# Score tiles in three places in the last steps, and a copy in place of a transfer for the last pair

## The chip, the cores and the metric

The kernel runs on one core of one Trainium2 chip. The metric is the device time of the whole program in microseconds (us). A core has TensorE (PE), VectorE (DVE), ScalarE (ACT), GpSimd (POOL) and SyncE (SP), each with a queue of its own that works strictly in program order. They meet only at semaphores. PE writes to PSUM, eight banks of 128 partitions by 512 float32.

## The reference

One transformer layer on a graph of 4096 nodes, with 128 channels, 8 heads of 16 and a hidden layer of 512. In each head every node attends to the nodes that the adjacency matrix marks.

```python
qkv = layer_norm(x, g1, be1) @ w_qkv                 # x: 4096 x 128
q, k, v = qkv.reshape(n, 3, HEADS, HEAD_DIM)[:, 0..2]
scores = einsum('nhd,mhd->hnm', q, k) * SCALE        # 8 x 4096 x 4096
attn = softmax(where(adj != 0, scores, -inf), axis=-1)
out = einsum('hnm,mhd->nhd', attn, v).reshape(n, DIM)
x = x + out @ w_proj + b_proj
h2 = layer_norm(x, g2, be2)
return x + gelu(h2 @ w1 + b1) @ w2 + b2
```

## The kernel before

**Tiling.** The queries are worked in 8 tiles of 512 (`TILES`), the heads in 4 pairs, the keys in 32 blocks of 128. A tile has 64 steps (`STEPS`): 16 steps for each pair, two key blocks in each step (`BLOCKS`, `block_of`). `run_iterations` runs `body(i, ...)` for i = 0 to 8; body 8 holds only what is left of tile 7. Its flags say what a body still does: b (there is a next tile), c (there is a tile), d (there was one before). Tile 7 has b false; body 8 has b and c false.

**A block.** PE writes the mask into two PSUM banks with four matmuls against an identity (`masks`, L1210), adds the scores of both heads with four matmuls (`scores`, L1225), ACT takes the exponential of both banks in one instruction (128x1024) into one of eight slots of `probs` (L794), and three steps later (`LAG`) PE multiplies by the values and adds up in `pv_ps` (`weigh_values`, L1118). In every odd step the first block is not masked by PE: POOL multiplies its exponentials with 0 or 1 (`mask_probs`, L565), and `weigh_values` waits for that.

**The scores' ring.** `score_ps` has four banks, two halves of two banks. All uses of it, blocks and small fills, are numbered as places (`SCORE_PLACE`, `ACT_PLACE`). The half is the place's number modulo 2, and PE waits in `score_turn` until ACT has taken the place two before (L1106). The fills are small products that ACT reads: the new queries, the shifts (the parts of the row maxima, L669), the second norm's transpose and the four up-projections. Which fills a body has depends on its flags: tile 7 has the shift fill of step 45, but not those of steps 53 and 61, and their places stay empty.

**The rows' ring.** `ring_ps` has three banks. PE writes row scores there (`row_scores`, L1054), DVE adds the adjacency row and takes the maximum (`row_maximum`, L832): four units in each step, 21 steps ahead of their use (`AHEAD`). So tile 7 has none in its steps 43 to 63. Some fills that DVE reads use this ring too. In tile 7 the last of them comes in step 38, and the next in step 5 of body 8.

**Order on PE in a step.** Two row units, then masks of both blocks and scores of both blocks (in an odd step: scores, masks, scores), two row units, an odd step's score fill, the weighing of three steps earlier, an even step's score fill, a row fill.

**Values of a pair.** When a pair's 16 steps are weighed, ACT copies `pv_ps` (`take_values`, L758): for an even pair to `halves[:, 0]`, for an odd one to `attn`. `move_values` then starts transfers from ACT's queue: for the even pair the upper 64 partitions go to `halves[0:64, 1]` (L764), for the odd pair both parts of `attn` go to `halves[64:128]` (L767, L768). POOL adds the two halves into `attn` (`sum_values`, L628) after `values_moved` has counted three transfers. For tile 7's last pair this happens in body 8, steps 3 and 5, and the rest of the layer follows in series: sums (L1152), reciprocals (L932), their broadcast (L1159), projection (L1167), second norm on DVE, transpose (L1137), up (L1142), Gelu (L749), down (L1176), output.

```python
for bank, to, (source, keys) in (...):
    last = nc.tensor.matmul(bank[to, :], ident_bf[keys, keys], mask_t[keys, source, :], start=True, stop=False)
last.then_inc(masks_set, 1)
```

Of the kernel before, what the change touches and what calls it, by code (L numbers as in the profile page):

```python
# [21 lines left out]
TILES = N // TILE  # L22
# [9 lines left out]
PAIRS = HEADS // 2  # L32
# [134 lines left out]

SCORES = Ring(0, ("score", SCORE_PLACE), ACT_PLACE, SCORE_PLACES)
ROWS = Ring(FIRST_UNITS, ("row", ROW_PLACE), DVE_PLACE, ROW_PLACES)


KEPT = [m for m in range(MB) if m % 4 == 3]
# [2 lines left out]
def pool_masked(p, m):  # L175

    return m in KEPT
# [62 lines left out]
def program(nc, x, adj, w_qkv, w_proj, b_proj, w1, b1, w2, b2, g1, be1, g2, be2, const, out):  # L240
    with ExitStack() as ctx:
# [132 lines left out]
        def made(ring, i, bcd, place):  # L374

            return ring.before(i) + ring.upto(bcd, place)

        def free(ring, i, bcd, place, turn):

            held = [p for p in ring.held(*bcd) if p <= place - turn and (place - p) % turn == 0]  # L380
            if bcd[1]:
                return made(ring, i, bcd, place - turn)
            return made(ring, i, bcd, held[-1]) if held else ring.before(i)

        block = ctx.enter_context(nc.Block())

# [101 lines left out]
        def _(pool):  # L488
# [134 lines left out]

            def sum_values(n, f):

                pool.wait_ge(values_moved, (n // 2) * (16 * 3))
                settled(pool)
                nc.gpsimd.tensor_tensor(attn[:, f, :], halves[:, 0, :], halves[:, 1, :], ALU.add).then_inc(attn_ready, 1)  # L628

# [35 lines left out]
        def _(act):  # L665
# [55 lines left out]

            def take_fill(i, par, bcd, g, what):

                half = 2 * (ACT_PLACE[g] % 2)
                bank = score_ps[:, half, :]
                act.wait_ge(score_full, made(SCORES, i, bcd, ACT_PLACE[g]))
                if what[0] == "q":
                    if bcd[2]:
                        act.wait_ge(gelu_done, i * FC)
                        act.wait_ge(q_stored, i * 32)  # L730
                    nc.scalar.copy(q_high[:, :], bank)
                    nc.scalar.copy(q_x[:, :], bank).then_inc(score_taken, 1)
                elif what[0] == "shift":
                    store_shift(q_stack[par if what[1] else 1 - par], bank, what[1], what[2]).then_inc(score_taken, 1)
                elif what[0] == "h2t":
                    nc.scalar.activation(h2T[:, :], bank, ACT.Identity, scale=gb[:, 2:3],  # L736
                                         bias=gb[:, 3:4]).then_inc(score_taken, 1)
                elif what[0] == "up" and bcd[1]:
                    f = what[1]
                    n = (i - 1) * FC + f  # L740
                    if f == 0:
                        act.wait_ge(q_done, min(i, TILES - 1))
                    if f >= 2:
                        act.wait_ge(gelu_done, n - 1)
                    nc.scalar.activation(hidden[:, f, :], bank, ACT.Identity, bias=b1_col[:, f:f + 1])
                    nc.scalar.activation(bent[f % 2], bank, ACT.Square, bias=b1_col[:, f:f + 1])\  # L746
                      .then_inc(score_taken, 1)
                elif what[0] == "up":
                    nc.scalar.activation(hidden[:, what[1], :], bank, ACT.Gelu_apprx_tanh,  # L749
                                         bias=b1_col[:, what[1]:what[1] + 1]).then_inc(score_taken, 1)  # L750
# [9 lines left out]
            def move_values(n, p):  # L760
# [4 lines left out]
                else:  # L765
                    act.wait_ge(values_moved, (n // 2) * (16 * 3) + 16)
                    act.dma_start(halves[64:128, 0, :], attn[64:128, p // 2, :]).then_inc(values_moved, 16)  # L767
                    act.dma_start(halves[64:128, 1, :], attn[0:64, p // 2, :]).then_inc(values_moved, 16)  # L768

            def body(i, par, b, c, d):  # L770
                bcd = b, c, d
                fills = fills_of(ACT_FILLS, b, c, d)
                for g in range(STEPS):
                    if g == X_STEP and d:
                        act.wait_ge(row_taken, ROWS.before(i))
                        act.dma_start(x_res[:, :, :], tile_of(x_view, i - 1)).then_inc(x_res_in, 16)
                    if b and g == XQ_STEP:
                        src = xnT_dram[i + 2] if isinstance(i, int) else \
                            xnT_dram[bass.ds(i + 2, 1)].rearrange("a p n -> p (a n)")
                        act.dma_start(xq[:, :], src).then_inc(xq_loaded, 16)  # L780
                    if d and g == LAG:
                        take_values(i * PAIRS - 1, PAIRS - 1, i * STEPS)
                        if not c:
                            move_values(i * PAIRS - 1, PAIRS - 1)
                    if c and g % QUARTER == LAG and g > QUARTER:
                        take_values(i * PAIRS + (g // QUARTER - 1), g // QUARTER - 1, i * STEPS + (g - LAG))
                    for n in range(BLOCKS):
                        if c:
                            if g >= SLOT_STEPS or not (isinstance(i, int) and i == 0):
                                act.wait_ge(pv_done, i * STEPS + (g - SLOT_STEPS + 1))  # L790
                            place = SCORE_PLACE[g, n]
                            act.wait_ge(score_full, made(SCORES, i, bcd, place))
                            half = 2 * (place % 2)
                            nc.scalar.activation(probs[:, (2 * g + n) % SLOTS, :],  # L794
                                                 score_ps[:, half:half + 2, :].rearrange("p a n -> p (a n)"),
                                                 ACT.Exp, scale=score_scale[:, 0:1]).then_inc(score_taken, 1)
                            if n == 0 and g % QUARTER == LAG and (g > QUARTER or d):

                                move_values(i * PAIRS + (g // QUARTER - 1), (g // QUARTER - 1) % PAIRS)
                    if g in fills:  # L800
                        take_fill(i, par, bcd, g, fills[g])
                    if d and c and g - 2 in UP_STEPS:
                        f = UP_STEPS.index(g - 2)
                        act.wait_ge(bent_done, 2 * ((i - 1) * FC + f) + 2)
                        nc.scalar.activation(bent[f % 2], bent[f % 2], ACT.Tanh).then_inc(tanh_done, 1)
                    if d and g == STORE_STEP:
                        act.wait_ge(row_taken, made(ROWS, i, bcd, DVE_PLACE[34]))
                        act.dma_start(tile_of(out_view, i - 1), rows2[:, :, :]).then_inc(out_stored, 16)
                    if d and g == SEEN_STEP:
                        act.wait_ge(out_stored, i * 16)  # L810
# [205 lines left out]
        def _(pe):  # L1016
# [85 lines left out]

            def score_turn(i, bcd, place):

                if place >= 2 or not (isinstance(i, int) and i == 0):
                    pe.wait_ge(score_taken, free(SCORES, i, bcd, place, 2))  # L1106

            def weigh_values(i, bcd, g):
# [14 lines left out]

            def act_fill(i, bcd, g, what):
                place = ACT_PLACE[g]
                bank = score_ps[:, 2 * (place % 2), :]
                score_turn(i, bcd, place)
                if what[0] == "q":
                    pe.wait_ge(xq_loaded, (i + 1) * 16)
                    last = nc.tensor.matmul(bank, wq_all[:, :], xq[:, :], start=True, stop=True)  # L1130
                elif what[0] == "shift":
                    pe.wait_ge(split_step, SPLIT_OPS * (neg_max_order(i + (what[1] == 0), what[1], what[2]) + 1))
                    last = transpose_shift(bank, what[2])
                elif what[0] == "h2t":
                    pe.wait_ge(ln2_applied, (i - 1) * (SUB + 1) + SUB)
                    for s in range(SUB):
                        last = nc.tensor.transpose(bank[:, 128 * s:128 * (s + 1)], rows2[:, s, :], ident[:, :])  # L1137
                elif what[0] == "up":
                    f = what[1]
                    if f == 0:  # L1140
                        pe.wait_ge(score_taken, made(SCORES, i, bcd, ACT_PLACE[H2T_STEP]))
                    last = nc.tensor.matmul(bank, w1_sb[:, 128 * f:128 * (f + 1)], h2T[:, :], start=True, stop=True)  # L1142
                last.then_inc(score_full, 1)
# [36 lines left out]
            def body(i, par, b, c, d):  # L1180
# [13 lines left out]
                def block(g, n):  # L1194

                    p, m = g // QUARTER, block_of(g, n)
                    half = 2 * (SCORE_PLACE[g, n] % 2)
                    return p, m, score_ps[:, half, :], score_ps[:, half + 1, :], pool_masked(p, m)

                def masks(g, n):  # L1200

# [86 lines left out]
```

## Time and profile before

| | us |
|---|---|
| median of 3 runs | 1713.71 (1713.29 to 1714.76) |
| the profiled execution | 1713.18 |
| its span | 1711.4 |
| PE busy | 1592.9 (93%) |
| DVE busy | 1418.5 (83%) |
| ACT busy | 1275.2 (75%) |
| POOL busy | 1167.7 (68%) |

The span is the time from the first to the last recorded instruction of one profiled execution. The profile has the mean exponential at 1112 ns, and its sections on 40 slices show PE at 9 tenths or more from the second slice to the last but two. A releaser in an arrow (`<-`) is what ended an engine's idle time.

### The profile page before, as it was taken

What the parts mean: (1) busy time and instruction counts of PE and PEld (TensorE: products, weight loads), DVE (VectorE), ACT (ScalarE), POOL (GpSimd) and SP (SyncE); (2) the same over time, 40 slices, a digit from 0 to 9 for tenths busy, and PEclk for the clock granted to TensorE, in tenths of its full rate; (3) what the DMA queues carried; (4) which work ended last, traced back from release to release, by engine and by line L of the source; (5) the groups of instructions that cost most, each with busy time, mean ns of one, the idle gap of its engine ahead of it and who ended that gap; (6) DMA issues with size and microseconds to landing.
All of it is one profiled execution on the core that took longest, in us unless ns stands there. A gap on an engine that the chain in (4) does not pass through costs nothing.

```text
span 1711.4 us, 46526 instructions
## 1 busy us (share of the span) xinstructions
PE 1592.9 (93%) x17016; PEld 496.3 (29%) x17016; DVE 1418.5 (83%) x4490; ACT 1275.2 (75%) x1393; POOL 1167.7 (68%) x1092
## 2 busy tenths in 40 slices
PE   6989999999999999999999999999999999999985
PEld 3422222323223232323223232232323232232313
DVE  6988989987999889987998879997899879998701
ACT  4647778787787878777786878778787877778782
POOL 4945587569856788568865689567875698567441
PEclk9969999999999999999999999999999999999998
DMA  8710047202560046401561035500462025500000
GB/s 215 183 50 2 17 137 132 63 5 69 146 134 2 5 129 132 88 5 39 147 123 43 5 104 134 112 5 14 146 128 63 5 77 146 102 2 5 14 4 19
DMA packets 178016, 126.15 MB, mean 74 GB/s; under 512 B 141006, under 2 KB 155215, under 8 KB 177788
## 3 DMA queue, kind: packets, MB, share of 16 engines
q1 hardware_dynamic: 163196, 108.49, 26.7%
q10 hardware_dynamic: 14592, 14.69, 3.3%
q8 instruction: 135, 2.21, 0.5%
q14 instruction: 93, 0.76, 0.1%
HBM read 77.25 MB, written 6.04 MB: 49 GB/s over the span
## 4 chain that ended last, share of the span: by engine, by line
PE 53%; ACT 22%; issue 14%; POOL 8%; DVE 2%; ACTq 1%; DMA 0%; POOLq 0%; DVEq 0%
ACT probs L794 20%; PE pv_ps L1118 15%; PE ring_ps L1054 10%; PE score_ps L1210 10%; PE score_ps L1225 9%; POOL probs L565 2%; PE ring_ps L1176 2%; PE score_ps L1142 2%; POOL k_stack L526 2%; ACT q_stack L669 1%; DVE masked_out L832 1%; PE ring_ps L1167 1%; PE ring_ps L1152 1%; PE ring_ps L1159 1%; POOL hidden L588 1%
## 5 line engine op out<-in xcount | busy, mean ns | idle before, releaser
L832 DVE CUSTOM_DVE_ANT_0 masked_out<-ring_ps,row_mask 128x512 bf16<-128x512 f32 x2048 | 1311.8, 688 | 138.3 <-PE ring_ps L1054 97.5
L794 ACT ACTIVATE probs<-score_ps,score_scale 128x1024 f32<-128x1024 f32 x1024 | 1089.9, 1112 | 346.9 <-PE score_ps L1225 334.3
L565 POOL TENSOR_TENSOR probs<-probs,keep 128x1024 int32<-128x1024 int32 x256 | 604.5, 2363 | 262.2 <-ACT probs L794 251.8
L1118 PE MATMUL pv_ps<-probs,v_ones 128*17 128x512 f32 x4096 | 544.6, 600 | 3.2 <-POOL probs L565 3.2
L1054 PE MATMUL ring_ps<-k_stack,q_stack 51*64 51x512 f16 x4096 | 488.8, 397 | 15.0 <-DVE row_max L832 13.8
L1225 PE MATMUL score_ps<-q_stack,k_stack 51*64 51x512 f16 x4096 | 375.2, 391 | 19.4
L1210 PE MATMUL score_ps<-mask_t,ident_bf 64*64 64x512 bf16 x3072 | 279.4, 388 | 39.1 <-ACT probs L794 20.0
L1054 PEld LDWEIGHTS ring_ps<-k_stack,q_stack 51*64 51x64 f16 x4096 | 169.3, 104 | 496.3 <-DVE row_max L832 448.5
L1225 PEld LDWEIGHTS score_ps<-q_stack,k_stack 51*64 51x64 f16 x4096 | 117.2, 104 | 217.6 <-PE score_ps L1210 186.2
L832 DVE DVE_READ_ACCUMULATOR2_ANT row_max<- 128x1 f32 x2048 | 170.1, 83 | 0.0
L1210 PEld LDWEIGHTS score_ps<-mask_t,ident_bf 64*64 64x64 bf16 x3072 | 93.0, 105 | 195.6 <-ACT probs L794 150.2
L504 POOL TENSOR_SCALAR row_mask<-row_mask 128x1024 bf16<-128x1024 bf16 x124 | 129.5, 1045 | 23.6 <-POOL row_mask L500 23.0
L500 POOL TENSOR_SCALAR row_mask<-adj_in 128x1024 bf16<-128x1024 uint32 x124 | 129.2, 1042 | 4.2 <-DVE row_max L832 2.1
L1118 PEld LDWEIGHTS pv_ps<-probs,v_ones 128*17 128x17 f32 x4096 | 72.4, 95 | 139.9 <-issue 72.9
L509 POOL TENSOR_SCALAR max_unit<-neg_max 128x4 f32<-128x4 f32 x64 | 12.7, 199 | 79.2 <-DVE neg_max L842 78.5
L932 DVE RECIPROCAL recip<-ring_ps 128x16 f32<-128x16 f32 x16 | 4.1, 258 | 73.4 <-PE ring_ps L1152 73.4
L669 ACT COPY q_stack<-score_ps 2x256 f16<-2x256 f16 x128 | 46.5, 363 | 9.2 <-PE score_ps L1021 6.9
L557 POOL TENSOR_SCALAR keep<-mask_t 128x512 int32<-128x512 bf16 x64 | 39.6, 618 | 5.4
L949 DVE TENSOR_TENSOR rows<-ring_ps,x_res 128x128 f32<-128x128 f32 x32 | 9.3, 292 | 40.7 <-PE ring_ps L1176 40.7
L1142 PE MATMUL score_ps<-h2T,w_sb 128*128 128x512 f32 x64 | 37.5, 679 | 2.4 <-ACT h2T L736 1.0
L574 POOL TENSOR_SCALAR q_x<-q_x 128x512 f32<-128x512 f32 x14 | 8.7, 621 | 45.1 <-ACT q_x L746 45.1
L702 ACT ACTIVATE hidden<-score_ps,part_coef 128x512 f16<-128x512 f32 x36 | 27.9, 775 | 13.9 <-PE score_ps L1079 11.2
(121 smaller groups left out, 809.0 us busy)
## 6 DMA issues: line engine op xcount, KB each, us to landing
adj_in<-adj SPq DMA_DIRECT2D x128, 512.0 KB, 4.2
halves<-attn ACTq DMA_DIRECT2D x32, 128.0 KB, 2.6
q_stack<-q_dram SPq DMA_DIRECT2D x42, 64.0 KB
mask_t<-row_mask SPq DMA_TRANSPOSE x128, 3.5
xq<-xnT_dram ACTq DMA_DIRECT2D x8, 256.0 KB, 2.6
halves<-halves ACTq DMA_DIRECT2D x16, 128.0 KB, 2.2
x_res<-x ACTq DMA_DIRECT2D x8, 256.0 KB, 4.6
out<-rows ACTq DMA_DIRECT2D x8, 256.0 KB, 5.5
```

Of the source, the lines that this page charges most:

```text
L500: nc.gpsimd.tensor_scalar(target, adj_in[:, half, :].bitcast(U32), 1.0, 0.0, ALU.min, ALU.max)\
L504: nc.gpsimd.tensor_scalar(target, target, BIG, -BIG, ALU.mult, ALU.add).then_inc(mask_done, 1)
L557: nc.gpsimd.tensor_scalar(keep[:, KEPT.index(m), :], mask_t[:, m, :], 1.0 / BIG, 1.0, ALU.mult, ALU.add)\
L565: nc.gpsimd.tensor_tensor(view, view, keep[:, KEPT.index(m), :].unsqueeze(1).broadcast_to([128, 2, TILE]), ALU.mult).then_inc(probs_masked, 1)
L669: last = nc.scalar.copy(stack[r:r + SHIFT_PARTS, p, 256 * jj:256 * (jj + 1)], bank.bitcast(F16)[r:r + SHIFT_PARTS, 0:256])
L794: nc.scalar.activation(probs[:, (2 * g + n) % SLOTS, :], score_ps[:, half:half + 2, :].rearrange("p a n -> p (a n)"), ACT.Exp, scale=score ...
L832: nc.vector.tensor_tensor_reduce(out=masked_out[:, place % 3, :], in0=ring_ps[:, place % 3, :], in1=row_mask[:, j, ch * 512:(ch + 1) * 512 ...
L1054: last = nc.tensor.matmul(ring_ps[64 * t:64 * (t + 1), place % 3, :], stack[rows, p, first:first + 64], k_stack[rows, p, ch, K_FIRST:], st ...
L1118: last = nc.tensor.matmul(pv_ps[32 * k:32 * k + HD + 1, :], v_ones[:, block_of(g, b), 2 * p + a, :], probs[:, (2 * g + b) % SLOTS, a * TIL ...
L1142: last = nc.tensor.matmul(bank, w1_sb[:, 128 * f:128 * (f + 1)], h2T[:, :], start=True, stop=True)
L1210: last = nc.tensor.matmul(bank[to, :], ident_bf[keys, keys], mask_t[keys, source, :], start=True, stop=False)
L1225: last = nc.tensor.matmul(bank[64 * t:64 * (t + 1), :], k_stack[rows, p, m // 4, at + 64 * t:at + 64 * (t + 1)], q_stack[par][rows, p, :], ...
```

## The change

From step 43 of tile 7 on, the 43 places of the scores (42 blocks and the shift fill of step 45, `LAST_PLACES`) go round three places: the two halves of `score_ps`, and the first two banks of `ring_ps`. A place's turn waits for the one three before it in that list. The first use of `ring_ps` waits for all row units to be taken. Every reader and writer gets its banks from `score_banks`.

For the last pair of tile 7, ACT copies from `pv_ps` directly to `halves[64:128]` in two copies of 64 partitions, of which the second reads partitions 0 to 63 and writes 64 to 127. No transfer is started, and POOL waits for `values_taken` instead of `values_moved`.

```diff
+LAST_PLACES = [p for p in SCORES.held(False, True, True) if p >= SCORE_PLACE[STEPS - AHEAD, 0]]
...
+        def in_last(i, place):
+            return isinstance(i, int) and i == TILES - 1 and place in LAST_PLACES
+
+        def score_banks(i, place):
+
+            half = place % 2
+            if in_last(i, place):
+                k = LAST_PLACES.index(place) % 3
+                if k == 2:
+                    return ring_ps[:, 0:2, :]
+                half = (LAST_PLACES[0] + k) % 2
+            return score_ps[:, 2 * half:2 * half + 2, :]
...
             def sum_values(n, f):
 
-                pool.wait_ge(values_moved, (n // 2) * (16 * 3))
+                if n < TILES * PAIRS:
+                    pool.wait_ge(values_moved, (n // 2) * (16 * 3))
+                else:
+                    pool.wait_ge(values_taken, n)
...
+            def take_last_values(n, seen):
+
+                act.wait_ge(values_moved, (n // 2) * (16 * 3) + 16)
+                act.wait_ge(pv_done, seen)
+                nc.scalar.copy(halves[64:128, 0, :], pv_ps[64:128, :])
+                nc.scalar.copy(halves[64:128, 1, :], pv_ps[0:64, :]).then_inc(values_taken, 1)
...
                     if d and g == LAG:
-                        take_values(i * PAIRS - 1, PAIRS - 1, i * STEPS)
-                        if not c:
-                            move_values(i * PAIRS - 1, PAIRS - 1)
+                        if c:
+                            take_values(i * PAIRS - 1, PAIRS - 1, i * STEPS)
+                        else:
+                            take_last_values(i * PAIRS - 1, i * STEPS)
...
             def score_turn(i, bcd, place):
 
-                if place >= 2 or not (isinstance(i, int) and i == 0):
+                k = LAST_PLACES.index(place) if in_last(i, place) else 0
+                if k == 2:
+                    pe.wait_ge(row_taken, ROWS.before(i + 1))
+                elif k > 2:
+                    pe.wait_ge(score_taken, made(SCORES, i, bcd, LAST_PLACES[k - 3]))
+                elif place >= 2 or not (isinstance(i, int) and i == 0):
                     pe.wait_ge(score_taken, free(SCORES, i, bcd, place, 2))
```

## Rows read from the trace of the kernel before

**Rows 1.** Windows, steps 43 to 63: start:end, length, busy of each engine, clock, DMA.
```profile
1620.00:1674.00 54.00, 45.11 (x460) 10.60 (x460) 0.52 (x3) 45.01 (x45) 24.18 (x13) 1.00 0.02 4
```
**Rows 2.** Timeline of ACT: start, length, what, in brackets the idle time before.
```profile
1623.55 4.29 ACT L794 ACTIVATE probs<-score_ps,score_scale 128x1024 f32<-128x1024 f32 x4 [0.80 <-PE score_ps L1225]
1627.86 0.74 ACT L669 COPY q_stack<-score_ps 2x256 f16<-2x256 f16 x2
1629.39 4.29 ACT L794 ACTIVATE probs<-score_ps,score_scale 128x1024 f32<-128x1024 f32 x4 [0.80 <-PE score_ps L1225]
...
1650.32 4.29 ACT L794 ACTIVATE probs<-score_ps,score_scale 128x1024 f32<-128x1024 f32 x4 [1.06 <-PE score_ps L1225]
...
1670.93 4.29 ACT L794 ACTIVATE probs<-score_ps,score_scale 128x1024 f32<-128x1024 f32 x4 [1.06 <-PE score_ps L1225]
```
**Rows 3.** Windows, one pair of steps (58 and 59).
```profile
1660.49:1665.58 5.09, 4.39 (x48) 1.05 (x44) 0.00 (x0) 4.24 (x5) 2.36 (x2) 1.00 0.00 0
```
**Rows 4.** Timeline of PE, ahead of step 44 and in one pair of steps.
```profile
1622.44 0.78 PE L1210 MATMUL score_ps<-mask_t,ident_bf 64*64 64x512 bf16 x8
...
1661.66 0.41 PE L1225 MATMUL score_ps<-q_stack,k_stack 51*64 51x512 f16 x4
1662.66 0.41 PE L1210 MATMUL score_ps<-mask_t,ident_bf 64*64 64x512 bf16 x4 [0.59 <-ACT probs L794]
1663.15 0.41 PE L1225 MATMUL score_ps<-q_stack,k_stack 51*64 51x512 f16 x4
1663.49 1.05 PE L1118 MATMUL pv_ps<-probs,v_ones 128*17 128x512 f32 x8
1664.47 0.78 PE L1210 MATMUL score_ps<-mask_t,ident_bf 64*64 64x512 bf16 x8
1665.08 0.65 PE L1225 MATMUL score_ps<-q_stack,k_stack 51*64 51x512 f16 x8
```
**Rows 5.** Timeline of PE in an earlier stretch, mask matmuls that waited for nothing.
```profile
1585.10 0.60 PE L1210 MATMUL score_ps<-mask_t,ident_bf 64*64 64x512 bf16 x8
1585.57 0.63 PE L1225 MATMUL score_ps<-q_stack,k_stack 51*64 51x512 f16 x8
```
**Rows 6.** Chain of waits (start, length, what), after the last weighing.
```profile
1677.77 0.59 ACT attn L758
...
1678.88 2.43 DMA halves<-attn
...
1681.47 1.27 POOL attn L628
...
1682.88 1.85 PE ring_ps L1152 x8
...
1685.16 1.93 PE ring_ps L1159 x32
```
**Rows 7.** Timeline of POOL, the last block that it masks.
```profile
1674.23 2.36 POOL L565 TENSOR_TENSOR probs<-probs,keep 128x1024 int32<-128x1024 int32 x1 [2.99 <-ACT probs L794]
```
**Rows 8.** Timeline of DVE, the last row unit.
```profile
1620.25 0.08 DVE L832 DVE_READ_ACCUMULATOR2_ANT row_max<- 128x1 f32 x1
```
**Rows 9.** Timeline of ACT, two copies from one bank in an earlier tile.
```profile
1395.77 0.58 ACT L731 CAST q_high<-score_ps 128x512 f16<-128x512 f32 x1 [0.21 <-PE score_ps L1130]
1396.25 0.59 ACT L732 COPY q_x<-score_ps 128x512 f32<-128x512 f32 x1
```
**Rows 10.** Windows after the last weighing; the column before the last two is the clock.
```profile
1680.00:1682.00 2.00, 0.00 (x0) 0.00 (x0) 0.00 (x0) 0.00 (x0) 0.53 (x1) 0.95 0.35 81
...
1688.00:1690.00 2.00, 1.83 (x14) 1.63 (x12) 1.00 (x4) 0.00 (x0) 0.00 (x0) 0.84 0.00 0
...
1692.00:1694.00 2.00, 0.00 (x0) 0.00 (x0) 1.65 (x11) 0.00 (x0) 0.00 (x0) 0.51 0.00 0
```
**Rows 11.** Timeline of PE, sums and broadcasts in an earlier tile.
```profile
1409.80 1.06 PE L1152 MATMUL ring_ps<-sum_sel,attn 128*128 128x4 f32 x8
1413.34 1.05 PE L1159 MATMUL ring_ps<-ident,recip 128*32 128x128 f32 x32
```

More of the change, by code:

```diff
@@ L722, in take_fill @@
             def take_fill(i, par, bcd, g, what):
-                half = 2 * (ACT_PLACE[g] % 2)
-                bank = score_ps[:, half, :]
+                bank = score_banks(i, ACT_PLACE[g])[:, 0, :]
                 act.wait_ge(score_full, made(SCORES, i, bcd, ACT_PLACE[g]))
@@ L792, in body @@
                             act.wait_ge(score_full, made(SCORES, i, bcd, place))
-                            half = 2 * (place % 2)
                             nc.scalar.activation(probs[:, (2 * g + n) % SLOTS, :],
-                                                 score_ps[:, half:half + 2, :].rearrange("p a n -> p (a n)"),
+                                                 score_banks(i, place).rearrange("p a n -> p (a n)"),
                                                  ACT.Exp, scale=score_scale[:, 0:1]).then_inc(score_taken, 1)
@@ L1125, in act_fill @@
                 place = ACT_PLACE[g]
-                bank = score_ps[:, 2 * (place % 2), :]
+                bank = score_banks(i, place)[:, 0, :]
                 score_turn(i, bcd, place)
@@ L1196, in block @@
                     p, m = g // QUARTER, block_of(g, n)
-                    half = 2 * (SCORE_PLACE[g, n] % 2)
-                    return p, m, score_ps[:, half, :], score_ps[:, half + 1, :], pool_masked(p, m)
+                    banks = score_banks(i, SCORE_PLACE[g, n])
+                    return p, m, banks[:, 0, :], banks[:, 1, :], pool_masked(p, m)
                 def masks(g, n):
```

## The prediction

> **What bounds the kernel now.** I read four views in this order. The windows of the trace first: the stretch that the change touches, the last 21 steps of tile 7, is the only one before the end in which DVE has next to nothing to do, and there PE is busy 45.1 of 54 us and ACT 45.0 of 54 [rows 1]. Neither is full, so they wait for each other. Then ScalarE's timeline [rows 2]: exponentials come in fours (two steps), 4.29 us each four, and ahead of each four ACT is idle, released by the last score matmul: 0.80 us as a rule, 1.06 us ahead of steps 54 and 62. One exponential lasts 1.11 us (the profile's table has the mean, 1112 ns), so four in 4.29 start every (4.29 - 1.11) / 3 = 1.06 us, and ACT alone would need 4 x 1.06 = 4.24 us for two steps. The two steps take 5.09 [rows 3].
>
> PE's timeline says why [rows 4]. With two places the mask matmuls of a step's second block, (g,1), need the place that the exponential just ended has read; only after them, in PE's program order, come the scores of (g,0), which ACT needs next. Ended exponential, 0.05 wait, four mask matmuls, two score matmuls and their drain make the 0.80. Ahead of steps 54 and 62 it is 1.06 because tile 7 skips the fills of steps 53 and 61: two blocks that follow each other then share one half, and both sets of masks wait. PE shows these waits as its own idle time (0.59, and more inside the groups), so it isn't the bound either: it is a handshake. Last, the chain of waits after the last exponential [rows 6]: copy of PSUM to attn, issue, transfer 2.43, sum on POOL, sums on PE.
>
> **The change part by part.** *Third place.* From step 43 on a block's scores need the exponential three places earlier, not two. The masks of (g,1) are then released one exponential, 1.06 us, earlier. ACT's next work was ready 0.80 after its last one ended; it is now ready 1.06 - 0.80 = 0.26 before. The idle time goes, if PE keeps up. PE's work without waits over two steps, from start to start: two weighings of values 0.98 each (1663.49 to 1664.47), eight masks 0.47 (1585.10 to 1585.57, where they waited for nothing [rows 5]), eight scores 0.58 (1665.08 to the next weighing at 1665.66), four scores of the odd step 0.24 (half of those 0.47), four masks with the drain that their scores wait for 0.49 (1662.66 to 1663.15), four scores 0.34 (1663.15 to 1663.49) [rows 4]. Sum 4.08, under 4.24. So ACT becomes the bound, 4.24 instead of 5.09: 0.85 a pair of steps. It is close: what is late next is PE, with 0.16 us to spare.
>
> POOL's masking of one block takes 2.36 of each 4.24 us and its result is used three steps later [rows 7]; not late. ACT's exponential also waits for the weighing four steps back, done over 1 us ahead by the same order.
>
> The ten idle times, one by one. Ahead of step 44: PE comes to these masks at 1622.44 only, after the weighing of step 40, so they gain just their wait: release of the second four at 1622.67 (half of 0.47 later) instead of about 1622.80, 0.14. Ahead of step 46: before, 44 to 46 starts 5.84 apart [rows 2] with the shift fill's two copies (0.74) between. The fill takes one of the three places, so the masks of (46,1) wait for the exponential of (45,1), and its 1.11 end plus 0.80 replaces copies of 0.74 that ran in that time: 3 x 1.06 + 1.11 + 0.80 = 5.09, gain 0.75. Ahead of 48, 50, 56, 58, 60: 0.85 each, 4.25. Ahead of 52, with the copy of pair 2's values in it, and PE's weighing of step 48 queued behind that copy: I take 0.80. Ahead of 54 and 62: 4.24 against 1.06 + 4.29 = 5.35, 1.11 each, 2.22. Sum 0.14 + 0.75 + 4.25 + 0.80 + 2.22 = 8.16 us.
>
> *Added waits.* The first use of the ring's banks, step 44's first block, waits on PE for all rows taken. DVE's last row operation ends at 1620.33 [rows 8], PE gets there at 1622.44 [rows 4]: 2.1 us of cover. Were DVE later than that, everything of step 44 would queue behind it on PE, once, by the lateness. No other engine waits for more semaphores than before. The index arithmetic is at build time: nothing.
>
> *After the last exponential.* The masking of step 63's first block on POOL (2.36) and the last weighing follow the exponential of that block as they do now, from 1674.23 to the copy at 1677.77 [rows 6, 7]: no gain, no loss; PE will idle some 1.4 us ahead of this weighing, since 60 to 62 are done earlier.
>
> *Copies in place of the transfer.* Removed: one copy of 128 rows, two issues, two transfers; now copy start to start of POOL's sum is 1681.47 - 1677.77 = 3.70 us [rows 6]. Added: two copies of 64 partitions by 512. The trace has no copy that writes other partitions than it reads. Bounds: as cheap as the pair of copies from one bank at L731 and L732, of which the second starts 0.48 later and lasts 0.59 [rows 9]; or twice that. An even cheaper one is excluded by the same row: they read the same 512 columns. I take the row: 0.48 + 0.59, and 0.07 for POOL's release (the last exponential but one ends at 1670.93 + 2 x 1.06 + 1.11 = 1674.16, its masking starts at 1674.23 [rows 2, 7]) = 1.14. Gain 2.56; at the dear end 1.5. The new wait for the older transfer is met: that one is issued in step 51, twelve steps earlier. x_res is on ACT's queue ahead of the copies as before, issued some 8 us earlier too, and not needed before the projection. With the transfer gone the late ones are POOL's sum and then PE, in series, as now.
>
> *Sum.* 8.16 + 2.56 = 10.7 us. The profiled execution took 1713.18 (span 1711.4 and 1.8 around it), so 1702.5 by its own time; it lies 0.5 below the median 1713.71, which is what a later measurement stands by, and from which I get 1703.0.
>
> **The granted clock, weighed.** In the touched stretch it stands at 1.00 (2.4 GHz) with PE idle for 0.6 us or more in each pair of steps [rows 1, 3]. It fell to 0.50 (1.2 GHz) at about 1681.9, within the 5.1 us in which PE did nothing between the last weighing and the sums [rows 6, 10], and the sums then took 1.85 where an earlier tile has 1.06, the broadcasts 1.93 where it has 1.05 [rows 6, 11]. With the change that idle stretch shrinks to 5.1 - 2.6 = 2.5 us. By a row, short idleness doesn't always save the clock: PE stopped at 1689.8 and it was down again at 1692.0 [rows 10]. So I leave the tail's clock as it is in the sum, and keep the difference as a rival: sums 0.79, the first half of the broadcasts and the first projection group (some 0.5 and 0.8), 2.1 us.
>
> The Trainium skill ("TensorE: Matmul & The Clock Gate", section on a second HAM failure mode) reports a kernel that cycled through PSUM banks and in which short idle times between groups of matmuls made the clock swing between its two levels. It speaks against a third place; by it the stage would run at 1.2 GHz in part, which is the slower rival below. The same page's section on HAM oscillation has longer gaps lower the clock, and a shorter one not: by that rule the tail would be the 2.1 us shorter, 1700.9. The trace agrees with neither yet: 1.00 throughout the handshake, and a fall after 2.2 us.
>
> **Rivals.** (a) PE becomes the bound: its busy row gives 4.39 a pair of steps, not 4.08 [rows 3]. That row counts modelled ends of matmuls that overlap, which speaks against it; for it, that my sum leaves only 0.16 and comes from rows in which PE often waited. Then each of ten pairs gives 0.15 less: 10.7 - 1.5 = 9.2, 1704.5. (b) The tail keeps 2.4 GHz through the sums: 12.8, 1700.9. (c) The third place buys nothing, since another wait ends at the same moment (POOL's masks in front of a weighing, or PE's order): only the copies are left, 1713.7 - 2.6 = 1711.1, which is no measurable change. Against it: the idle times ahead of the exponentials are released by score matmuls in all ten cases. (d) The other side: PE, now running to a different beat, is granted 1.2 GHz in the stage. Its 4.08 become 8.2 a pair against 5.09 now: plus 3.1 for each pair so hit, up to 10 x 3.1 - 2.6 = 28 us slower, 1742. It decides from three of the ten pairs on (3 x 3.1 = 9.3 lost against 7 x 0.82 + 2.6 = 8.3 won). Against it: PE gets busier, from 4.08/5.09 to 4.08/4.24, where 1.00 was granted already.
>
> **How the numbers follow.** Forecast 1703.0: 0.64; (a) 0.16; (b) 0.11; (c) 0.06; (d) 0.03. About 0.2% (3.4 us) is what a measurement of this kernel can tell from no change. Faster: forecast, (a), (b) and a little over, 0.92; same: (c) and part gains, 0.05; slower 0.03. The forecast's own spread is about 1 us either way (where the clock rises again in the last stage moves by chance, and the three runs of before span 1.5). The range takes (b) at its low end, 1700.8, and above (a) the dear copies (1.1) and some of the phase: 1706.0.
>
> **What would show it.** After: exponentials of steps 46 to 63 start 1.06 apart with idle time only around the shift fill and the pair's copy, and pairs of steps take 4.24 in place of 5.09; PE idles on masks that wait for an exponential, not ACT on scores. First to last of those exponentials shortens by about 8. Two copies 0.5 apart, then POOL's sum 1.1 after the first one's start. PE's idle stretch ahead of the sums is 2.5. The prediction is wrong if fours of exponentials still have gaps of 0.3 or more, if the granted clock in the stage is under 1.00, or if the copies across partitions last much over 0.6.

## The result and the profile after

The changed kernel takes 1702.17 us (median of 6 runs, 1699.25 to 1704.14) beside 1713.55 of the kernel before (6 runs, 1711.34 to 1714.78). The ratio is 0.993, 95% interval 0.992 to 0.994. A second set on another occasion (below, `e5_after_again`) gave 0.992, 0.9908 to 0.9933. The forecast was 1703.0.

The profiled execution of the changed kernel took 1704.14 (span 1702.3), the slowest of its six. The two profiled spans differ by 9.1 us, the medians by 11.4. What makes these two figures differ lies outside the changed stretch, so I set marks at places that both traces have.

| mark to mark, us | before | after | gain |
|---|---|---|---|
| span's start to the exponential of step 42 | 1618.46 | 1620.19 | -1.73 |
| from there to the first copy of the last pair | 59.31 | 49.90 | 9.41 |
| from there to POOL's sum | 3.70 | 1.34 | 2.36 |
| from there to PE's sums | 1.41 | 1.41 | 0.00 |
| from there to the span's end | 28.52 | 29.46 | -0.94 |

The first and the last line are the same program in both kernels. They scatter from run to run, and both are looked at further below. The two changed parts gained 11.8 us.

ScalarE's timeline of the changed kernel stands below against [rows 2]. The first exponential of step 44 still waits 0.69. After it the brackets with idle time are gone; what interrupts is the shift fill's copy and the copy of pair 2's values. `ring_ps` is now read in every third place.

```profile
1620.19 4.29 ACT L820 ACTIVATE probs<-score_ps,score_scale 128x1024 f32<-128x1024 f32 x4 [0.86 <-PE score_ps L1256]
1625.17 1.11 ACT L820 ACTIVATE probs<-ring_ps,score_scale 128x1024 f32<-128x1024 f32 x1 [0.69 <-PE ring_ps L1256]
...
1629.33 0.74 ACT L689 COPY q_stack<-score_ps 2x256 f16<-2x256 f16 x2
...
1659.16 1.11 ACT L820 ACTIVATE probs<-ring_ps,score_scale 128x1024 f32<-128x1024 f32 x1
1660.17 2.11 ACT L820 ACTIVATE probs<-score_ps,score_scale 128x1024 f32<-128x1024 f32 x2
1662.16 1.12 ACT L820 ACTIVATE probs<-ring_ps,score_scale 128x1024 f32<-128x1024 f32 x1
1663.21 2.12 ACT L820 ACTIVATE probs<-score_ps,score_scale 128x1024 f32<-128x1024 f32 x2
```

Windows of two pairs of steps, against [rows 3] (after the length come the busy times of PE, PE's weight loads, DVE, ACT and POOL, each with its number of instructions, then the clock): 4.05 us in place of 5.09, ACT busy all the time, PE for 3.98 of it, clock 1.00.

```profile
1647.02:1651.07 4.05, 3.98 (x48) 1.05 (x44) 0.00 (x0) 4.05 (x6) 2.36 (x2) 1.00 0.02 4
1659.16:1663.21 4.05, 3.97 (x48) 1.05 (x44) 0.00 (x0) 4.05 (x6) 2.37 (x2) 1.00 0.01 4
```

PE's timeline of one such pair, against [rows 4]. No line has idle time in brackets, and each starts where the one before releases it: 0.98, 0.24, 0.24, 0.25, 0.24, 0.31, 0.98, and so on. From weighing to second next weighing 1657.17 to 1661.22 is 4.05.

```profile
1657.17 1.05 PE L1149 MATMUL pv_ps<-probs,v_ones 128*17 128x512 f32 x8
1658.15 0.41 PE L1241 MATMUL ring_ps<-mask_t,ident_bf 64*64 64x512 bf16 x4
1658.39 0.39 PE L1241 MATMUL score_ps<-mask_t,ident_bf 64*64 64x512 bf16 x4
1658.64 0.41 PE L1256 MATMUL ring_ps<-q_stack,k_stack 51*64 51x512 f16 x4
1658.88 0.39 PE L1256 MATMUL score_ps<-q_stack,k_stack 51*64 51x512 f16 x4
1659.19 1.05 PE L1149 MATMUL pv_ps<-probs,v_ones 128*17 128x512 f32 x8
1660.17 0.41 PE L1256 MATMUL score_ps<-q_stack,k_stack 51*64 51x512 f16 x4
1660.42 0.39 PE L1241 MATMUL ring_ps<-mask_t,ident_bf 64*64 64x512 bf16 x4
1660.88 0.41 PE L1256 MATMUL ring_ps<-q_stack,k_stack 51*64 51x512 f16 x4
1661.22 1.05 PE L1149 MATMUL pv_ps<-probs,v_ones 128*17 128x512 f32 x8
```

The chain of waits after the last weighing, against [rows 6]: the transfer is gone, and two copies stand in its place, 0.59 apart.

```profile
1670.09 0.58 ACT halves L793
1670.68 0.59 ACT halves L794
...
1671.43 1.27 POOL attn L648
...
1672.84 1.47 PE ring_ps L1183 x8
```

### The profile page after: what moved, and what is told of

Same layout as the page of the kernel before. It is cut to its first block, busy times and chain, and to the rows that moved or that the text cites. A ratio compares the mean times of both kernels' runs of the same rounds, so it can differ in the third digit from the quotient of the medians.

```text
span 1702.3 us, 46524 instructions
## 1 busy us (share of the span) xinstructions
PE 1588.7 (93%) x17016; PEld 496.5 (29%) x17016; DVE 1419.3 (83%) x4490; ACT 1274.2 (75%) x1394; POOL 1167.4 (69%) x1092
## 4 chain that ended last, share of the span: by engine, by line
PE 52%; ACT 22%; issue 14%; POOL 8%; DVE 2%; ACTq 1%; DMA 1%; SPq 0%; POOLq 0%; DVEq 0%
ACT probs L820 20%; PE pv_ps L1149 15%; PE ring_ps L1080 10%; PE score_ps L1241 9%; PE score_ps L1256 9%; POOL probs L582 2%; PE ring_ps L1207 2%; PE score_ps L1173 2%; POOL k_stack L543 2%; ACT q_stack L689 1%; DVE masked_out L858 1%; PE ring_ps L1198 1%; PE ring_ps L1183 1%; PE ring_ps L1190 1%; POOL row_mask L517 1%
## 5 line engine op out<-in xcount | busy, mean ns | idle before, releaser
L820 ACT ACTIVATE probs<-score_ps,score_scale 128x1024 f32<-128x1024 f32 x1010 | 1075.6, 1112 | 338.5 <-PE score_ps L1256 324.4
L1256 PE MATMUL score_ps<-q_stack,k_stack 51*64 51x512 f16 x4040 | 370.4, 391 | 18.9
L1241 PE MATMUL score_ps<-mask_t,ident_bf 64*64 64x512 bf16 x3028 | 274.9, 387 | 34.1 <-ACT probs L820 15.5
L722 ACT ACTIVATE hidden<-score_ps,part_coef 128x512 f16<-128x512 f32 x36 | 28.0, 777 | 14.5 <-PE score_ps L1105 11.8
```

Of the source, the lines that this page charges most:

```text
L820: nc.scalar.activation(probs[:, (2 * g + n) % SLOTS, :], score_banks(i, place).rearrange("p a n -> p (a n)"), ACT.Exp, scale=score_scale[: ...
L1256: last = nc.tensor.matmul(bank[64 * t:64 * (t + 1), :], k_stack[rows, p, m // 4, at + 64 * t:at + 64 * (t + 1)], q_stack[par][rows, p, :], ...
```

## The experiments

After this profile two accounts of the stage were open. The chain of waits of the changed kernel runs over ACT's exponentials almost without a break; by it ACT is the bound. PE's timeline has no wait either, and its starts add up to the same 4.05. So the first set takes the parts one by one and loads each engine in turn.

**Third place alone.** The changed kernel with `take_values` and `move_values` back, and POOL waiting for `values_moved` again.

```diff
-                        if c:
-                            take_values(i * PAIRS - 1, PAIRS - 1, i * STEPS)
-                        else:
-                            take_last_values(i * PAIRS - 1, i * STEPS)
+                        take_values(i * PAIRS - 1, PAIRS - 1, i * STEPS)
+                        if not c:
+                            move_values(i * PAIRS - 1, PAIRS - 1)
...
```

> The changed kernel with the transfers of the last pair put back: only the third place is new. My account, from the traces of before and after: the third place gives 9.5 to 9.7 us from the exponential of step 44 on (two steps in 4.05 instead of 5.09), the copies 2.4. So about 9.6 us below the kernel before, 1704.0. Rival (third place hidden, the copies and the clock made the gain): under 3 us, 1711. The prediction's own figure for this part was 8.2, 1705.4.

Measured: 1703.8 beside 1714.56, ratio 0.9941 (0.9929 to 0.9954), a gain of 10.8 by the medians, with an interval of about 7.9 to 12.2. In its trace the exponential of step 42 starts at 1620.97 and the copy at 1670.80, which is 49.83 against 59.31 before: 9.5. From that copy on the series is as before, with the transfer of 2.43:

```profile
1670.80 0.59 ACT attn L774
...
1671.92 2.43 DMA halves<-attn
...
1674.51 1.27 POOL attn L645
```

**Copies alone.** The changed kernel with two places throughout.

```diff
-            return isinstance(i, int) and i == TILES - 1 and place in LAST_PLACES
+            return False
```

> The kernel before with only the two copies in place of the last pair's transfers, the scores in two places throughout. Sum by my account: from the start of the first copy to POOL's sum 1.34 instead of 3.70, so 2.4 us below the kernel before, 1711.2. If the shorter idle stretch of PE keeps the clock at 2.4 GHz through the sums, up to 2 us more. Rival (the tail's clock gives the gain back, as 0.9 us did in the profiled execution of the changed kernel): under 1 us.

Measured: 1711.45 beside 1714.56, ratio 0.998 (0.9971 to 0.9989): 3.1 by the medians, with an interval of about 1.9 to 5.0. In the trace step 42 to the copy takes 59.37, the copy to PE's sums 2.75 instead of 5.11. The two parts don't touch each other: by the traces 9.5 in one stretch, 2.36 in the other, 11.8 together. The medians of the two parts add up to 13.9, where both at once gave 11.4 and 12.9; with intervals this wide that is no contradiction.

**More work for PE.** The added call runs the same four matmuls once more and raises no semaphore.

```diff
                     if c and pool_step(g):
+                        if i == TILES - 1 and g >= STEPS - AHEAD + 2:
+                            scores(g, 0, False)
                         scores(g, 0)
```

> The changed kernel, in which PE computes the scores of the first block of each odd step from 45 to 63 of the last tile twice, to the same values: four more matmuls, 0.24 us, in each pair of steps. If PE is what now sets 4.05 a pair (its starts follow each other without a wait), a pair takes 4.29, 10 pairs 2.4 us more. If ACT sets it and PE has time to spare, a pair stays at 4.05.

Measured: a pair of steps takes 4.27 (one execution, 1705.6). From step 42 to the copy 51.41, against 49.90. That is 1.5 more in all, not the 2.4 expected. The marks of both traces show where the rest is: seven pairs grow by 0.21 to 0.23 each, and three don't, namely the pair with the shift fill, one of the two around the copy of pair 2's values, and the last. In those PE idles in the changed kernel, for 0.54, 0.61 and 0.87, and the added matmuls fill part of that. The regular pair is what the two accounts differ in. Windows of one pair of this kernel, from weighing to weighing:

```profile
1654.52:1658.79 4.27, 4.20 (x53) 1.02 (x49) 0.00 (x0) 4.13 (x5) 2.37 (x1) 1.00 0.00 0
```

**Less work for ACT.** From step 46 on the exponentials take only the first head of a block; those of the second head are left out.

```diff
-                            nc.scalar.activation(probs[:, (2 * g + n) % SLOTS, :],
+                            size = TILE if i == TILES - 1 and g >= STEPS - AHEAD + 3 else 2 * TILE
+                            nc.scalar.activation(probs[:, (2 * g + n) % SLOTS, 0:size],
...
```

> The changed kernel, in which the exponentials from step 46 of the last tile on take only the first of the two heads (128x512 instead of 128x1024, about 0.6 us instead of 1.1); the second head's are left out. If PE sets the pace, a pair of steps stays at 4.05 within 0.05. If ACT's exponentials set it (the chain of waits runs over them), a pair shortens to what PE needs, which is then below 4.05 by 0.2 or more.

Measured: 4.05 a pair, to the hundredth, while ACT is busy for 2.64 of it and waits 1.12 and 0.28 for scores (one execution, 1698.78). Windows of one pair, and ScalarE's timeline of a later one:

```profile
1643.94:1647.99 4.05, 3.97 (x48) 0.90 (x45) 0.00 (x0) 2.64 (x5) 2.37 (x2) 1.00 0.02 4
```

```profile
1652.00 0.69 ACT L821 ACTIVATE probs<-score_ps,score_scale 128x512 f32<-128x512 f32 x1 [1.12 <-PE score_ps L1257]
1652.59 0.68 ACT L821 ACTIVATE probs<-ring_ps,score_scale 128x512 f32<-128x512 f32 x1
1653.54 1.39 ACT L821 ACTIVATE probs<-score_ps,score_scale 128x512 f32<-128x512 f32 x2 [0.27 <-PE score_ps L1257]
```

That settles it: PE sets the pace of the stage in the changed kernel, at 4.05. ACT is right behind it, with exponentials 1.00 to 1.01 apart, some 4.02 a pair; this is why the chain of waits, which goes back over ACT as long as ACT starts one instruction at the end of another, names the wrong engine. The two experiments agree: 0.24 more of PE's work lengthens the pair by 0.22, and 1.4 less of ACT's leaves it as it was.

**The changed kernel again,** the control of the second set.

> The changed kernel itself, timed beside the three others of this set on one chip. The two parts alone gave 1703.8 and 1711.4 beside 1714.6; if they add up, 1714 - 9.6 - 2.4 (with the scatter of the kernel before on this chip), 12 us below the kernel before. If the tail takes back part of what the copies gave, 10 to 11.

Measured: 1701.44 beside 1714.29, ratio 0.992 (0.9908 to 0.9933), so 12.9. From sums to the end 28.8 here, where the first profiled execution had 29.5. In this execution the clock had fallen before the sums, within an idle stretch of 2.9. A mean of 0.78 over the two microseconds from 1668 means that it fell at about 1669.1, 2.2 us after the last weighing's end at 1666.9. Windows around it:

```profile
1668.00:1670.00 2.00, 0.21 (x2) 0.24 (x2) 0.00 (x0) 0.21 (x1) 1.26 (x1) 0.78 0.00 0
1670.00:1672.00 2.00, 1.63 (x8) 1.54 (x8) 0.26 (x1) 0.00 (x0) 0.00 (x0) 0.50 0.00 0
```

**A busy PE in the tail.** Matmuls that nobody reads, in program order ahead of the serial ones: 11 ahead of the sums, 24 ahead of the second norm's transpose, 3 after it.

```diff
+BUSY = {5: 11, 18: 24, 20: 3}
...
+            def busy(count):
+                for _ in range(count):
+                    nc.tensor.matmul(score_ps[:, 1, :], ident_bf[:, :], mask_t[:, 0, :], start=True, stop=True)
...
+                    if not c and g in BUSY:
+                        busy(BUSY[g])
```

> The changed kernel, in which PE also runs matmuls whose results nobody reads (128x512 bf16 into a bank of score_ps that is free there): 11 ahead of the sums of body 8, 24 ahead of the second norm's transpose, 3 after it. By the trace of the changed kernel PE idles 2.8, 5.7 and 1.0 us there, and the granted clock is 0.50 from 1673.6 to 1680.0 and from 1683.8 to 1693.8. If these idle stretches are what lowers the clock, it stays at 1.00 to the end, and the serial matmuls shorten: sums 1.46 to 1.06, broadcasts 0.9 less in part, projection 3.7 to about 2.1, transpose 1.1 to 0.66, up-projections 6.5 to about 4.2: 4 to 5 us less than the changed kernel, and a smaller scatter of the runs. If the clock's fall has another cause, no gain, or a loss where the added matmuls delay the next ones.

Measured: 1695.33 beside 1714.29, ratio 0.9892 (0.9877 to 0.9907), 6.1 below the control's median. The scatter did not shrink (1694.98 to 1699.73). The clock stays at 1.00 to PE's last matmul, where the changed kernel had 0.74 on the mean. From PE's sums to the span's end 23.7 instead of 28.8 and 29.5. The ten profiled executions without such matmuls, kernel before and experiments included, have 27.5 to 29.5 there, so the gain by traces is 3.8 to 5.8. Windows of the tails, first of the changed kernel, then of this one:

```profile
1670.00:1702.30 32.30, 18.43 (x100) 13.19 (x100) 8.06 (x36) 5.97 (x8) 2.52 (x2) 0.74 0.03 9
```

```profile
1666.00:1692.00 26.00, 21.18 (x144) 12.56 (x138) 8.01 (x36) 5.97 (x8) 2.53 (x2) 1.00 0.02 7
```

PE's timeline of the up-projections, the largest piece, in the changed kernel and in this one:

```profile
1688.03 6.51 PE L1173 MATMUL score_ps<-h2T,w_sb 128*128 128x512 f32 x8 [0.96 <-ACT h2T L755]
```

```profile
1681.54 3.89 PE L1176 MATMUL score_ps<-h2T,w_sb 128*128 128x512 f32 x8 [0.31 <-ACT h2T L758]
```

**DVE sums the last pair.** ACT makes one copy, DVE adds from PSUM.

```diff
-                nc.scalar.copy(halves[64:128, 0, :], pv_ps[64:128, :])
...
+                nc.vector.tensor_tensor(attn[0:64, FOURS - 1, :], halves[0:64, 0, :], halves[0:64, 1, :], ALU.add)\
...
+                nc.vector.tensor_tensor(attn[64:128, FOURS - 1, :], pv_ps[64:128, :], halves[64:128, 1, :], ALU.add)\
...
```

> The changed kernel, in which the sum of the last pair is made by DVE: the lower half of attn from the two halves that lie ready, the upper half from PSUM and the one copy of partitions 0 to 63 to 64 to 127. From the trace of the changed kernel: first copy to the end of POOL's sum is 1.34 + 1.27 = 2.61 us; one copy of 0.58 and a DVE addition of about 0.69 with their releases make 1.4. So 1.2 us less than the changed kernel, if the series after it doesn't change; the shorter idle stretch of PE ahead of the sums (1.6 instead of 2.8 us) may keep the clock up for longer, up to 2 us more. If the clock rather than the series sets the tail, no measurable difference from the changed kernel.

Measured: 1700.64 beside 1714.29, ratio 0.9915 (0.9901 to 0.9928). By the medians 0.8 below the control, which these runs can't tell from nothing. The trace can: copy to PE's sums 1.52 instead of 2.75, so 1.2 as worked out. The timeline of this kernel:

```profile
1669.38 0.58 ACT L793 COPY halves<-pv_ps 64x512 f32<-64x512 f32 x1 [2.75 <-PE pv_ps L1161]
1670.06 0.69 DVE L1006 TENSOR_TENSOR attn<-pv_ps,halves 64x512 f32<-64x512 f32 x1 [25.82 <-ACT halves L793]
```

**Step 63 masked by PE.**

```diff
-                    return p, m, banks[:, 0, :], banks[:, 1, :], pool_masked(p, m)
+                    return p, m, banks[:, 0, :], banks[:, 1, :], pool_masked(p, m) and not last_step(g)
...
```

> The changed kernel, in which step 63's first block is masked by PE and not by POOL. In the changed kernel's trace PE idles 0.87 us ahead of the last weighing, for POOL's 2.36 us. Without it the last weighing follows step 62's; four more masks cost PE 0.24 before. Some 0.8 us less from the weighing of step 60 to the copy, which the medians can hardly show: 0.5 to 1.0 below the changed kernel's 1701.4 to 1702.2. If another wait ends at the same time (the exponential of step 63's second block), under 0.2.

Measured: 1700.94 beside 1713.76, ratio 0.9925 (0.9912 to 0.9939), again no difference from the changed kernel that medians tell. In the trace, step 42 to the copy is 49.04 against 49.90: 0.86. The four weighings now run without a gap:

```profile
1663.63 3.63 PE L1149 MATMUL pv_ps<-probs,v_ones 128*17 128x512 f32 x32
```

**All three of these.** The busy tail has 5 matmuls ahead of the sums here, not 11.

> The changed kernel with DVE's sum, with step 63's first block masked on PE instead of POOL, and with the matmuls nobody reads (5, 24 and 3). POOL's masking, 2.36 us, then no longer stands between the last exponentials and the last weighing: the weighing of step 63 follows the one of step 62, some 0.8 us earlier, less 0.24 for four more mask matmuls. Together: 1.2 + 0.6 + 4.5, about 6 us below the changed kernel, 1696. If the clock doesn't answer to idle stretches, 1.8 below.

Measured: 1695.28 beside 1714.29, ratio 0.9883 (0.9869 to 0.9896), the fastest of all by the ratio, if not by a margin that the medians show over the busy tail alone (1695.33). By marks it is: from the exponential of step 42 to the span's end 74.3 us, against 76.4 of the busy tail, 81.5 of the control, 82.1 of the changed kernel and 92.9 of the kernel before. It had the later start of step 42 of the two (1619.57 against 1616.85), which is the part that no edit touches.

**Two copies of the same partitions.** The second copy reads partitions 64 to 127 as well, so the move of partitions 0 to 63 is left out.

```diff
-                nc.scalar.copy(halves[64:128, 1, :], pv_ps[0:64, :]).then_inc(values_taken, 1)
+                nc.scalar.copy(halves[64:128, 1, :], pv_ps[64:128, :]).then_inc(values_taken, 1)
```

> The changed kernel, in which the second of the two copies reads partitions 64 to 127 as the first does, so that the move of partitions 0 to 63 is left out. In the changed kernel the second copy starts 0.59 after the first, with nothing of the overlap of 0.10 that two copies of one bank had in the kernel before. If reading other partitions than the copy before is what takes the overlap away, it starts 0.48 after it here. If copies of 64 partitions never overlap, or writing the same tile is the cause, 0.59 again.

Measured: the second copy starts 0.49 after the first, where the pair in [rows 9] has 0.48 (one execution, 1703.39). The copy that reads other partitions costs the overlap, 0.10 us, and lasts 0.58 as the straight one does. The edit changes two things at once, though: the second copy reads the partitions that the copy before it read, and it no longer moves them. The shift fill's two copies speak for the first: each writes the partitions that it reads, but not those of the other, and two of 0.36 take 0.74, with no overlap. No run separates the two.

```profile
1669.45 0.58 ACT L793 COPY halves<-pv_ps 64x512 f32<-64x512 f32 x1 [2.75 <-PE pv_ps L1149]
1669.94 0.58 ACT L794 COPY halves<-pv_ps 64x512 f32<-64x512 f32 x1
```

## Why the prediction was right, and where a step of it failed

The time and the two mechanisms came out: a handshake between PE and ACT that a third place undoes (8.2 forecast, 9.4 measured), and a transfer replaced by copies (2.6 forecast, 2.4 measured). What came out otherwise is the engine that is the bound afterwards. The total is nearer than its parts: the stage gave 1.2 us more and the copies 0.2 less, and single runs of one kernel spread over 3.4 and 4.9 us, so that the median came within 0.8 us of the forecast is partly luck. Point by point:

- *A pair of steps, 5.09 to 4.24.* It became 4.05. The step that failed is "four in 4.29 start every (4.29 - 1.11) / 3 = 1.06 us". That divides by three intervals, as if nothing in the four waited. The merged line hides a wait. Cut into narrow windows, ScalarE's timeline of the kernel before has the first, second and fourth of such a four:

```profile
1660.49 1.11 ACT L794 ACTIVATE probs<-score_ps,score_scale 128x1024 f32<-128x1024 f32 x1 [0.80 <-PE score_ps L1225]
1661.50 1.11 ACT L794 ACTIVATE probs<-score_ps,score_scale 128x1024 f32<-128x1024 f32 x1
...
1663.67 1.11 ACT L794 ACTIVATE probs<-score_ps,score_scale 128x1024 f32<-128x1024 f32 x1
```

  The second starts 1.01 after the first; the fourth 2.17 after the second, where two intervals of ACT's own pace make 2.02: it was held 0.15 by its scores. ACT's own pace is 1.00 to 1.01, also behind the values' copy.
- *PE's work 4.08, "0.16 to spare".* The sum was right (4.05 measured), its use was wrong: beside ACT's real 4.02 PE's sum is the larger, so PE and not ACT is the bound. So rival (a)'s mechanism happened, PE the bound, but not at its price: the busy row's 4.39 counts overlapping ends, as was said against it. A regular pair gained up to 1.04 and not 0.85. Over the five regular pairs (ahead of 48, 50, 56, 58 and 60) that is 5.15 in place of 4.25, 0.9 us of the 1.25 that the stage gave beyond the forecast. The rest is the step ahead of 62 (1.30, forecast 1.11) and, less, those ahead of 46, 52 and 54.
- *Steps 44 and 46.* The idle time ahead of step 44 fell from 0.80 to 0.69, forecast 0.14 less. From 44 to 46 the starts are 4.93 apart (1625.17 to 1630.10), forecast 5.09, before 5.84.
- *The 0.80.* It is made up with "two score matmuls". A block has four, and ACT waits for all; no number of the sum hangs on this.
- *Copies, 1.14 to POOL's sum.* It was 1.34. Two things were mis-sized by 0.1 each: the overlap of the copies, lost as the last experiment shows, and the release of POOL, 0.17 and not 0.07. The 0.07 had the same false 1.06 in it: the exponential that POOL waits for ended at about 1674.05, not 1674.16.
- *The last weighing still waits for POOL.* Right, with 0.87 of idle time ahead of it; 1.4 was said.

```profile
1668.91 1.05 PE L1149 MATMUL pv_ps<-probs,v_ones 128*17 128x512 f32 x8 [0.87 <-POOL probs L582]
```

- *Added waits.* Nothing waited on the row units: PE wrote into `ring_ps` at 1624.17, straight after the weighing before it.
- *The clock.* The slower rival (d) didn't happen: 1.00 in the whole stage. The Trainium skill ("TensorE: Matmul & The Clock Gate", on a second HAM failure mode) has a kernel whose clock swings as it cycles through PSUM banks, with PE idle for short times in between. This stage doesn't agree with it: with two places PE idled 0.59 and more in each pair, with three it idles only at the shift fill and at the pair's copy (0.54 and 0.61), and the clock stood at 1.00 both times. Rival (b), the shorter idle stretch that keeps the clock up, is not decided by the idle stretch's length: with 2.9 us ahead of the sums (2.5 forecast), they took 1.46 in one profiled execution of the changed kernel, 1.84 in the other and 1.03 in the kernels with the copies alone and with step 63 masked by PE. The sum was right to leave it out, and 0.9 us of the first profiled execution went the other way.
- *What would show it.* "PE idles on masks, not ACT on scores" was wrong: neither idles.

What stays open in part: the scatter of the runs. From the span's start to step 42 the twelve profiled executions, of programs that are the same up to there, range from 1616.85 to 1620.97. Most of it is there before the first exponential, which starts between 116.69 and 122.06:

```profile
116.69 2.12 ACT L823 ACTIVATE probs<-score_ps,score_scale 128x1024 f32<-128x1024 f32 x2 [9.70 <-PE score_ps L1263]
122.06 2.12 ACT L816 ACTIVATE probs<-score_ps,score_scale 128x1024 f32<-128x1024 f32 x2 [9.70 <-PE score_ps L1252]
```

It goes with TensorE's granted clock over the first 100 us: 1.00 for the earliest, 0.95 for the two at 118.5, 0.93 for the six from 119.4 to 119.6, 0.90 and 0.91 for the three from 121.1 on. A second place is in the middle of the kernel. In five of the twelve, the kernel before among them, the clock falls to 0.50 between 937.5 and 940.6 us and is back at 1.00 by 941 to 944, which delays all that follows by 1.2 to 1.4 us. In the kernel before PE paused for 0.70 and 0.28 us just ahead of it, and the changed kernel's second profile has the same pauses (0.69 and 0.28) and kept 1.00. What decides it no run shows. Windows of the kernel before, then of the changed kernel's second profile:

```profile
938.00:941.00 3.00, 3.00 (x24) 0.50 (x16) 1.40 (x7) 1.23 (x3) 2.62 (x4) 0.50 0.00 0
938.00:941.00 3.00, 2.92 (x40) 0.67 (x32) 2.38 (x9) 2.17 (x4) 2.63 (x4) 1.00 0.00 0
```

## What to carry to other kernels

The mean interval of instructions that a timeline merges into one line can hold a wait, so it is an upper bound of the engine's own interval: divide the line into single starts before one engine's floor is worked out from it, since a floor that is 5% off names the wrong engine where two are close. When two engines hand a small ring to and fro and both show idle time, add up each one's work from start to start; the larger of the two sums is the shortest period that an additional place can reach. A chain of waits follows whichever engine ran without a gap, so cut one engine's work and look whether the period moves.

## What the runs showed that I had not expected

The serial tail is bound in good part by PE's clock: keeping PE occupied there, with results that nobody reads, shortens the series from PE's sums to the end from 28.8 or 29.5 to 23.7 us; by the medians that is 6.1 us, about half of what the whole change gave. The clock fell 2.2 us after PE's last matmul in one execution, and held 1.00 through PE's pauses of 0.2 to 0.9 us in the busy tail. The Trainium skill ("TensorE: Matmul & The Clock Gate", section on HAM oscillation) has idle stretches lower the clock; by the busy tail the trace agrees.

Two ScalarE copies that follow each other overlapped by 0.09 to 0.10 us where they read the same partitions, and not at all where the second read others and moved them. That is two pairs with the overlap; the pair without it stands 0.59 apart in all seven profiles that have it.
